# A graph-attention kernel on one core: VectorE makes the destination lanes and codes of two groups of edges at once

## What is computed

```python
def _gat_layer(x, src, dst, W, a_src, a_dst, b, heads, ch, concat):
    n = x.shape[0]
    h = (x @ W).reshape(n, heads, ch)
    alpha_src = jnp.sum(h * a_src, axis=-1)
    alpha_dst = jnp.sum(h * a_dst, axis=-1)
    e = alpha_src[src] + alpha_dst[dst]
    e = jnp.where(e > 0, e, NEG_SLOPE * e)
    alpha = _segment_softmax(e, dst, n)
    msg = h[src] * alpha[:, :, None]
    out = jax.ops.segment_sum(msg, dst, num_segments=n)
    out = out.reshape(n, heads * ch) if concat else out.mean(axis=1)
    return out + b
```

## Time and profile before

| what | value |
|---|---|
| median of 3 runs | 8928.67 us (8913.6 to 8929.7) |
| the profiled execution, whole | 8916.15 us |
| its span, first to last instruction | 8914.5 us |
| first attention layer (4060 to 6440 us of the span) | 2380 us, DVE busy 2269.61 us |
| second attention layer (6560 to 8840 us of the span) | 2280 us, DVE busy 1582.16 us, POOL 1718.94 us |
| mean granted TensorE clock | 0.765 of full speed |

### The profile page before, as it was taken

How to read it: one execution, slowest core, us unless ns; L and a number is a source line. 1 busy time by engine, 2 the same in 40 slices (tenths; PEclk the granted TensorE clock), 3 DMA queues, 4 the chain that set the end, 5 groups by cost and what they waited for, 6 DMA issues and landing times.

```text
span 8914.5 us, 232214 instructions
## 1 busy us (share of the span) xinstructions
PE 6375.9 (72%) x50562; PEld 5197.4 (58%) x50563; DVE 6392.5 (72%) x27688; ACT 4848.8 (54%) x11854; POOL 6136.1 (69%) x7562
## 2 busy tenths in 40 slices
PE   2466666666599999985777777777647777777775
PEld 2366656665588888863444444444445665556664
DVE  7799833333267767757999999999957777777776
ACT  4133333333245555535767667677647777777775
POOL 0377777777777777735777777777637777777775
PEclk9988888888799999986888888888755555555555
DMA  4232222222233333312222222222521111111114
GB/s 141 52 63 62 62 63 62 63 62 62 60 92 85 86 86 85 86 30 59 55 54 55 54 54 55 55 54 54 49 23 28 28 28 28 28 28 28 28 28 27
DMA packets 990660, 491.49 MB, mean 55 GB/s; under 512 B 830674, under 2 KB 841604, under 8 KB 990276
## 3 DMA queue, kind: packets, MB, share of 16 engines
q0 software_dynamic: 168832, 302.29, 15.6%
q1 hardware_dynamic: 701892, 169.48, 10.4%
q10 hardware_dynamic: 119840, 18.68, 1.3%
HBM read 356.53 MB, written 151.48 MB: 57 GB/s over the span
## 4 chain that ended last, share of the span: by engine, by line
issue 25%; DVE 20%; PE 19%; POOL 18%; DMA 7%; ACT 6%; DVEq 3%; ACTq 1%; POOLq 0%; SPq 0%
POOL z_s L637 13%; POOL arena L687 5%; DMA arena<-table,arena 5%; PE ps_all L959 5%; PE ps_all L969 5%; PE ps_all L982 3%; ACT arena L823 3%; PE ps_all L979 2%; DVE shift L1528 2%; DVE arena L1487 2%; DVE arena L1532 2%; PE ps_all L1066 1%; ACT arena L855 1%; DVE arena L1573 1%; DMA z_s<-arena 1%
## 5 line engine op out<-in xcount | busy, mean ns | idle before, releaser
L687 POOL DMA_INDIRECT arena<-table,arena x3616 | 3471.7, 960 | 1504.4 <-issue 982.6
L637 POOL DMA_INDIRECT z_s<-arena x1660 | 1592.1, 959 | 849.9 <-issue 477.5
L1090 PE MATMUL ps_all<-arena 128*128 128x132 f32 (+1 forms) x7232 | 1561.4, 384 | 1.8 <-DVE acc L1590 1.8
L1090 PEld LDWEIGHTS ps_all<-arena 128*128 128x128 f32 x7232 | 1384.9, 284 | 2.7 <-issue 2.6
L823 ACT ACTIVATE arena<-lanes_b,arena 128x128 bf16<-128x128 bf16 x3616 | 1147.1, 387 | 415.6 <-DVE arena L1461 414.4
L1487 DVE TENSOR_REDUCE arena<-ps_all 128x2 f32<-128x1024 f32 x904 | 1098.9, 1216 | 15.5 <-PE ps_all L1107 15.5
L1066 PE MATMUL ps_all<-ident_b,arena 128*128 128x128 bf16 x3616 | 472.3, 273 | 789.1 <-DMA arena<-table,arena 522.6
L1107 PE MATMUL ps_all<-arena,pick 128*128 128x512 bf16 x2260 | 971.0, 523 | 72.5 <-DVE arena L1487 72.1
L847 ACT ACTIVATE arena<-ps_all 28x512 bf16<-28x512 bf16 (+1 forms) x904 | 522.6, 578 | 718.5 <-PE ps_all L1066 718.5
L742 ACT ACTIVATE arena<-ps_all 18x512 f32<-18x512 f32 x415 | 243.3, 586 | 1212.0 <-PE ps_all L946 1192.5
L1066 PEld LDWEIGHTS ps_all<-ident_b,arena 128*128 128x128 bf16 x3616 | 291.1, 120 | 942.7 <-DVE arena L1474 528.8
(11 more groups left out here) (259 smaller groups left out, 16141.0 us busy)
## 6 DMA issues: line engine op xcount, KB each, us to landing
arena<-z_s SPq DMA_DIRECT2D x452, 264.0 KB, 2.7
arena<-table,arena POOLq DMA_INDIRECT x3616
arena<-rec_d SPq DMA_DIRECT2D x1660, 10.0 KB
z_s<-arena POOLq DMA_INDIRECT x1660
rec_d<-in_rec ACTq DMA_DIRECT2D x1, 16160.0 KB, 58.8
arena<-ids_d SPq DMA_DIRECT2D x904, 4.0 KB
arena<-pos_d SPq DMA_DIRECT2D x830, 0.5 KB
arena<-pos_d ACTq DMA_DIRECT2D x830, 0.5 KB
```

The source lines that it names most:

```text
L637: pool.indirect_dma_start(z_s, bass.IndirectOffsetOnAxis(ap=slot[:, g.slot(SLOTS), u:u + 1], axis=0), z_out[:, g.slot(SLOTS), u, :], None) ...
L687: pool.indirect_dma_start(g_rows[:, r, u * step + CODE_WORDS:(u + 1) * step], None, tables[n], bass.IndirectOffsetOnAxis(ap=ids[:, r, 0, u ...
L1090: mm = pe.matmul(ps[6][:, 0:out_w], a_hot_f[:, g.slot(4), u, :], g_msg[:, g.slot(4), u * out_w:(u + 1) * out_w], start=(u == 0), stop=(u = ...
```

## The change

In every second step (when the next group's number inside the turn is odd) `edge_codes` gets two groups, t and t+1 (`ahead = of(-1)`), and each of its operations covers both; in the other steps it does nothing. The two slots lie side by side, so the operations are 128x8, 128x8, 128x128, 128x64 and 128x64. L1458 and L1461 were tensor-with-pointer operations (TENSOR_SCALAR) and become TENSOR_TENSOR, with two columns of `first_node` broadcast along the four columns of a group. Each operation adds two to a semaphore of its own: `a_lane_ready`, `neg_lane_ready`, `bits_ready`, `low_code_ready`, `high_code_ready`. The waits on DVE are those of the later group. SP waits for two semaphores where it waited for one, PE too; ACT waits for `neg_lane_ready`.

```diff
-                        sp.wait_ge(S("a_lane_ready"), g.back(SLOTS).done(2))
+                        sp.wait_ge(S("a_lane_ready"), g.back(SLOTS).done())
+                        sp.sem_inc(S("sp_go"), 1)
+                        sp.wait_ge(S("neg_lane_ready"), g.back(SLOTS).done())
...
-                        act.wait_ge(S("a_lane_ready"), g.done(2))
+                        act.wait_ge(S("neg_lane_ready"), g.done())
...
-                        pe.wait_ge(S("code_ready"), g.done(2))
+                        pe.wait_ge(S("low_code_ready"), g.done())
+                        pe.wait_ge(S("high_code_ready"), g.done())
...
-                def edge_codes(g):
+                def edge_codes(g, h):
...
-                    dve.wait_ge(S(f"ids_in_{r}"), g.uses(SLOTS, 16))
-                    dve.tensor_scalar(lane_int[:, g.slot(4), :], ids[:, r, 1, :], first, None, ALU.subtract).then_inc(S("a_lane_ready"), 1)
-                    if g.back(4).exists():
-                        dve.wait_ge(S("a_hot_ready"), g.back(4).done())
-                    dve.tensor_scalar(neg_lane[:, g.slot(4), :], ids[:, r, 1, :], -1.0, first, ALU.mult, ALU.add).then_inc(S("a_lane_ready"), 1)
+                    first = first_node[:, bass.ds(g.at, 2)].unsqueeze(2).broadcast_to([P, 2, U])
+                    for k in (g, h):
+                        dve.wait_ge(S(f"ids_in_{k.slot(SLOTS)}"), k.uses(SLOTS, 16))
+                    dve.tensor_tensor(lane, node, first, ALU.subtract).then_inc(S("a_lane_ready"), 2)
+                    if h.back(4).exists():
+                        dve.wait_ge(S("a_hot_ready"), h.back(4).done())
+                    dve.tensor_tensor(minus, first, node, ALU.subtract).then_inc(S("neg_lane_ready"), 2)
...
+                    dve.tensor_tensor(bits.rearrange("p k u c -> p (k u) c"),
+                                      lane.rearrange("p k u -> p (k u)").unsqueeze(2).broadcast_to([P, 2 * U, CODE]),
+                                      bit_masks.unsqueeze(1).broadcast_to([P, 2 * U, CODE]), ALU.bitwise_and).then_inc(S("bits_ready"), 2)
...
+                    dve.tensor_scalar(codes[:, :, :, 0:CODE // 2], bits[:, :, :, 0:CODE // 2], 0.0, -BIG, ALU.is_equal, ALU.mult
+                                      ).then_inc(S("low_code_ready"), 2)
+                    dve.tensor_scalar(codes[:, :, :, CODE // 2:CODE], bits[:, :, :, CODE // 2:], 0.0, -BIG, ALU.not_equal, ALU.mult
+                                      ).then_inc(S("high_code_ready"), 2)
...
-                    codes, large, shifts = edge_codes(of(0)), largest_shares(of(3)), new_shifts(of(4))
+                    ahead = of(-1)
+                    codes = edge_codes(of(0), ahead) if ahead is not None and ahead.off % 2 == 1 else iter(())
+                    large, shifts = largest_shares(of(3)), new_shifts(of(4))
```

More of the change, by code:

```diff
@@ L1446, in _ @@
                 buckets = Rounds(dve, mybir.EngineType.DVE, bucket_of, NT - 1, SLOTS, 2 * SLOTS)
-                def edge_codes(g):
+                def edge_codes(g, h):
                     if g is None:
                         return
-                    r = g.slot(SLOTS)
-                    codes = g_rows[:, r, 0:U * step].bitcast(BF16).rearrange("p (u w) -> p u w", u=U)
-                    bits = lane_bits[:, g.slot(4)]
-                    first = first_node[:, bass.ds(g.at, 1)]
-                    dve.wait_ge(S(f"ids_in_{r}"), g.uses(SLOTS, 16))
-                    dve.tensor_scalar(lane_int[:, g.slot(4), :], ids[:, r, 1, :], first, None, ALU.subtract).then_inc(S("a_lane_ready"), 1)
-                    if g.back(4).exists():
-                        dve.wait_ge(S("a_hot_ready"), g.back(4).done())
-                    dve.tensor_scalar(neg_lane[:, g.slot(4), :], ids[:, r, 1, :], -1.0, first, ALU.mult, ALU.add).then_inc(S("a_lane_ready"), 1)
+                    r, q = g.slot(SLOTS), g.slot(4)
+                    codes = g_rows[:, r:r + 2, 0:U * step].bitcast(BF16).rearrange("p k (u w) -> p k u w", u=U)
+                    lane, minus = lane_int[:, q:q + 2], neg_lane[:, q:q + 2]
+                    bits = lane_bits[:, q:q + 2]
+                    node = ids[:, r:r + 2, 1, :]
+                    first = first_node[:, bass.ds(g.at, 2)].unsqueeze(2).broadcast_to([P, 2, U])
[5 more added lines that the diff above has]
+                    dve.tensor_tensor(minus, first, node, ALU.subtract).then_inc(S("neg_lane_ready"), 2)
@@ L1462, in edge_codes @@
                     yield
-                    dve.wait_ge(S("a_lane_ready"), g.done(2))
-                    dve.tensor_tensor(bits, lane_int[:, g.slot(4), :].unsqueeze(2).broadcast_to([P, U, CODE]),
-                                      bit_masks.unsqueeze(1).broadcast_to([P, U, CODE]), ALU.bitwise_and).then_inc(S("bits_ready"), 1)
+                    dve.wait_ge(S("a_lane_ready"), h.done())
+                    dve.tensor_tensor(bits.rearrange("p k u c -> p (k u) c"),
+                                      lane.rearrange("p k u -> p (k u)").unsqueeze(2).broadcast_to([P, 2 * U, CODE]),
+                                      bit_masks.unsqueeze(1).broadcast_to([P, 2 * U, CODE]), ALU.bitwise_and).then_inc(S("bits_ready"), 2)
@@ L1466, in edge_codes @@
                     yield
-                    if g.back(SLOTS).exists():
-                        dve.wait_ge(S("turned"), g.back(SLOTS).done())
-                    dve.wait_ge(S("bits_ready"), g.done())
-                    dve.tensor_scalar(codes[:, :, 0:CODE // 2], bits[:, :, 0:CODE // 2], 0.0, -BIG, ALU.is_equal, ALU.mult
-                                      ).then_inc(S("code_ready"), 1)
-                    dve.tensor_scalar(codes[:, :, CODE // 2:CODE], bits[:, :, CODE // 2:], 0.0, -BIG, ALU.not_equal, ALU.mult
-                                      ).then_inc(S("code_ready"), 1)
+                    if h.back(SLOTS).exists():
+                        dve.wait_ge(S("turned"), h.back(SLOTS).done())
```

1 line of the change is left out of this document (added).

## The result

The changed kernel takes 8903.37 us in the median (8889.92 to 8908.02, 10 runs) against 8928.91 us (10 runs) of the kernel before beside it: a ratio of 0.9973, 95% interval 0.9964 to 0.9981. The forecast was 94 us, and the time lies above the range. The profile after is of an execution of 8889.92 us, the fastest of the ten and 13.5 us under their median.

A forecast was written before the change was run, and what follows sets the result against it. DVE was taken to bound layer one and POOL layer two. 54 turns x (42.14 - 40.4) = 94 us, with 0 from layer two, taken from 8928.67 gave 8835 us; range 8808 to 8879.

The forecast's parts named there:

- The step that loses its codes: Layer one, the DVE step of a pair without codes, lanes and bits: gains 0.50 us, bounds 0.40 to 0.56.
- The stall behind L1522: Layer one, step without codes: a dependent operation follows too closely, so 0.06 us of the gain turn into a stall.
- The step with two groups' codes: Layer one, the DVE step with the wide operations: costs 0.02 us more, bounds -0.06 to +0.16.
- DVE's turn: Layer one, eight steps on DVE: from 42.14 to 40.2 us, between 39.7 and 41.2.
- The part of the turn that is lost at its start stays: Layer one, DVE at the start of a turn: the time lost there is unchanged, while four pairs gain 1.92 us.
- The larger counts: 40.4: Layer one: DVE and POOL ask for nearly the same time, POOL's 40.4 us a turn counts; gain 94 us.
- Layer two: Second attention layer: POOL's turn of 40.4 us stays the bound, DVE has idle time; gain 0 us.
- third rival: POOL's gathers last longer beside DVE's new two-operand operations; sign: gathers over 0.95 us in layer two; slower, chance 0.04.
- The waits that are added: DVE's wait for the later group's ids and second semaphores on PE and SP: cost nothing.
- DVE stays the bound: Rival, layer one: wide operations or stalls cost more, turn 40.65 to 41.2 us, 8849 to 8879 us; chance 0.25.
- Another wait takes the place: Rival, layer one: DVE waits for ACT or PE instead, gain within 18 us, 8911 to 8947 us; chance 0.06.
- The gathers stretch: Rival, POOL: new two-operand DVE operations lengthen gathers; 0.1 us a step takes back 90 us; slower, chance 0.04.

The follow-up runs named there:

- c_one_input: Changed kernel on chip B, message multiplication replaced by a one-input TENSOR_REDUCE, weights left out: 8850.07 us, 0.9954 of the kernel before.
- c_three: Changed kernel on chip B with three gathers for a group in place of four, from a layer's ninth group on: 8386.81 us, one run.
- d_psum: Changed kernel on chip C; ACT writes the exponentials a second time into PSUM, the message multiplication reads its weights there: 9032.41 us, 1.0114 of the kernel before.
- c_halves: Changed kernel on chip B with the message multiplication in two operations of half the elements: 8877.35 us, 0.9985 of the kernel before.
- a_three: Changed kernel on chip A with three gathers for a group in place of four, from a layer's ninth group on: 10375.74 us, one run.
- a_one_input: Changed kernel on chip A, message multiplication replaced by a one-input TENSOR_REDUCE, weights left out: 12249.50 us, 1.0005 of the kernel before.

## Why the prediction was wrong, point by point

**The step that loses its codes: right.** Expected 0.50 us; in the steady part of a turn these steps are 4.55 to 4.61 us in c_one_input, 0.43 to 0.49 under the 5.04 of before. The stall behind L1522 was expected to cost 0.06. The stalls are larger, and partly elsewhere: from start to start L1560 takes 0.11 us for the 0.08 of old, and L1525, ahead of L1592, 0.19 for 0.07 (medians). The old L1535 took 0.13 ahead of the codes and takes 0.07 now, which gives some of it back.

**The step with two groups' codes: right in the middle of the turn.** Timeline of DVE in the changed kernel, around bits, codes and lanes, in the middle of a turn:

```profile
5520.84 0.18 DVE L1479 TENSOR_SCALAR arena<-arena 128x64 bf16<-128x64 int32 x1
5520.94 0.18 DVE L1481 TENSOR_SCALAR arena<-arena 128x64 bf16<-128x64 int32 x1
5521.04 0.14 DVE L1520 TENSOR_SCALAR arena<-dst_parts 128x12 bf16 x1
...
5525.75 0.22 DVE L1464 TENSOR_TENSOR arena<-arena,first_node 128x8 int32<-128x8 int32 x1
5525.89 0.15 DVE L1467 TENSOR_TENSOR arena<-first_node,arena 128x8 f32<-128x8 int32 x1
5525.97 0.16 DVE L1560 TENSOR_TENSOR arena<-arena,ps_all 128x16 f32<-128x16 f32 x1
...
5526.56 0.29 DVE L1470 TENSOR_TENSOR arena<-arena,bit_masks 128x128 int32<-128x128 int32 x1
5526.77 0.16 DVE L1568 TENSOR_TENSOR arena<-arena,ps_all 128x16 f32<-128x16 f32 x1
```

From start to start: codes 0.10 each (expected 0.11), the lanes 0.14 and 0.08 here and 0.10 and 0.08 in the median (0.08), bits 0.21 (0.20). The prices drawn from neighbouring rows held to 0.02 us.

**DVE's turn: 40.8 to 41.0 and not 40.2. This is the first step that failed.** The sum took every pair of the turn for a steady pair. Median step lengths of layer one, from L1520 to L1520:

| step of the turn | 0 | 1 | 2 | 3 | 4 | 5 | 6 | 7 |
|---|---|---|---|---|---|---|---|---|
| before | 5.54 | 4.91 | 5.05 | 5.04 | 5.04 | 5.04 | 5.04 | 6.48 |
| c_one_input | 5.77 | 4.56 | 5.20 | 4.55 | 5.03 | 4.61 | 5.03 | 5.93 |

The steps without codes gave 0.35, 0.49, 0.43 and 0.55, together 1.82 of the 2.00 counted. The others cost +0.23, +0.15 and twice -0.01, together 0.36 where 0.08 was counted, and all of it in steps 0 and 2 (step 2 is at 5.08 in the changed kernel itself). "The part of the turn that is lost at its start stays" was wrong: the stop stays, but in step 0 the lanes save nothing. In the kernel before, behind the stop at 5410.86:

```profile
5411.08 0.16 DVE L1515 TENSOR_TENSOR arena<-arena,alpha_d 128x4 f32<-128x4 f32 x1
5411.32 0.23 DVE L1458 TENSOR_SCALAR arena<-arena,first_node 128x4 int32<-128x4 int32 x1
5411.46 0.22 DVE L1461 TENSOR_SCALAR arena<-arena,first_node 128x4 f32<-128x4 int32 x1
5411.59 0.17 DVE L1553 TENSOR_TENSOR arena<-arena,ps_all 128x16 f32<-128x16 f32 x1
```

In the changed kernel, behind the stop at 5515.24:

```profile
5515.46 0.16 DVE L1522 TENSOR_TENSOR arena<-arena,alpha_d 128x4 f32<-128x4 f32 x1
5515.76 0.17 DVE L1464 TENSOR_TENSOR arena<-arena,first_node 128x8 int32<-128x8 int32 x1
5515.94 0.17 DVE L1467 TENSOR_TENSOR arena<-first_node,arena 128x8 f32<-128x8 int32 x1
5516.05 0.17 DVE L1560 TENSOR_TENSOR arena<-arena,ps_all 128x16 f32<-128x16 f32 x1
```

The first operations behind the stop were slow before as well (L1515 0.24 us, where it takes 0.07 in mid-turn). Now L1522 holds DVE for 0.30 us and L1464 for 0.18. From L1515 to L1553 were 0.51 us, from L1522 to L1560 are 0.59: 0.08 more, where the same change saves 0.10 in mid-turn. What they wait for there, the trace doesn't name. With 40.80 in place of 40.4 the forecast would have been some 22 us smaller; by c_one_input, layer one without held gathers is 66.1 us shorter than in the profile of before, not 94.

**"The larger counts: 40.4": the second failure, and the larger.** It took POOL's turn as a fixed 40.4 us, with every gather at 1.26 us whatever DVE does beside it; a price for gathers that meet the multiplication stood nowhere in the sum. 71.2 us of held time against 22.0 is the row that says no; c_one_input puts its price at 46.7 us in layer one and 8.7 in layer two, 51 us of the median. With the 28 us of the step before that is 79 us for 69 missing. The two prices come from different chips and single profiles; where the 10 us too many belong isn't shown.

**Layer two: 0, and it was +6.3 us.** POOL was its bound, as said, and that is why nothing hides a held gather there. With 128x256 elements the multiplication occupies DVE for 0.34 us and holds a gather by up to 0.2: between 6600 and 8700 us 64 gathers of the changed kernel start 0.1 or 0.2 us behind it (median durations 1.14 and 1.04), and none of the kernel before. That is the sign that the prediction had named for its third rival, gathers longer than 0.95 in layer two.

**The waits that are added: nothing, right.** No wait of DVE for ids stands in the table of waits of layer one.

**The rivals.** *DVE stays the bound* described layer one half-way: its 40.65 to 41.2 us is DVE's turn as c_one_input and c_three show it, but in the changed kernel POOL, and not DVE, sets the turn. *Another wait takes the place* failed: L1580 never waits for ACT in the changed kernel. *The gathers stretch* was the right mechanism with the wrong actor and the wrong price. The prediction looked at the new operations with two SBUF operands, of 0.08 to 0.2 us; they hold little (of 69 gathers that start during L1470 in layer one, three take over 1.0 us; in c_one_input 12 of 67, at most 1.07). The one that holds the gathers is the old message multiplication, which the change doesn't touch. And it dismissed the rival with "the gathers take 0.95" of layer two, although has 1.04 and 1.07, and the trace of before has 22 gathers over 1.1 us and a longest of 1.47 in layer one. Each of the 22, and the 1.07, started 0.5 us or less behind L1573; the 1.04 started 0.09 us behind L1585, another operation with two operands in SBUF. That one look, at the longest gather rather than at the usual one, would have shown what a gather costs that starts at the wrong time, and that the change takes away the even step that kept the others out of it.

The Trainium skill ("SBUF — State Buffer", section "Who interferes with whom") states the rule that the prediction had weighed: a DVE instruction with two inputs in SBUF and a GpSimd instruction that reads SBUF exclude each other. This case's runs agree in one direction: a gather that starts during the multiplication takes up to 1.51 us for 0.95 with two inputs in SBUF, 0.95 to 0.96 with one (c_one_input) or with the other in PSUM (d_psum). In the other direction they show nothing: with a gather under way the multiplication takes 0.60 us from its start to the next, as without one.

## What to carry to other kernels

When a change makes an engine's steps uneven or shortens them, look at how its long operations with two SBUF operands lie against the gathers of POOL, and read the longest gathers, not the median. A gain measured on one chip can be none on another: here it was 25 us in two comparisons and nothing in the third. Two engines whose periods match can be locked in a harmless position, and the profile before then shows nearly nothing of what a slide costs. A loop's first steps are to be priced by their own rows, since there a saving can vanish that is real in the steady steps.

## What the runs showed of the hardware that was not expected

- The multiplication holds a gather only if it *starts* while the multiplication runs, and by that operation's rest (1.48 us at 0.03 us behind it, 1.34 at 0.19). A gather that is under way is not disturbed (0.95 us at 5524.51). Two such operations in a row act as one: 1.57 us.
- Two operands in SBUF are not the whole condition. The wide code operations L1479 and L1481 of the changed kernel have one, and of 45 gathers that start during L1479 in layer one 22 take over 1.0 us. POOL, then DVE:

```profile
4245.59 1.09 POOL L689 DMA_INDIRECT arena<-table,arena  x1 [0.30 <-issue]
```

```profile
4245.56 0.18 DVE L1479 TENSOR_SCALAR arena<-arena 128x64 bf16<-128x64 int32 x1
4245.66 0.18 DVE L1481 TENSOR_SCALAR arena<-arena 128x64 bf16<-128x64 int32 x1
4245.76 0.15 DVE L1520 TENSOR_SCALAR arena<-dst_parts 128x12 bf16 x1
```

  The gather is 0.14 us too long, held until about the end of L1481. The price here is small, 2.8 us in layer one; why these operations hold it wasn't tested.
- In layer two of the changed kernel DVE stops for some 4 us at the start of a turn (4.05 in the median, 1.47 before). Timeline of DVE, starts of steps:

```profile
7417.18 0.17 DVE L1520 TENSOR_SCALAR arena<-dst_parts 128x3 bf16 x1
...
7426.93 0.17 DVE L1520 TENSOR_SCALAR arena<-dst_parts 128x3 bf16 x1 [4.40 <-issue]
...
7431.29 0.16 DVE L1520 TENSOR_SCALAR arena<-dst_parts 128x3 bf16 x1
...
7434.11 0.16 DVE L1520 TENSOR_SCALAR arena<-dst_parts 128x3 bf16 x1
```

  The queue that brings instructions moved 329 packets in the whole of that execution, and 65 before (the page's third part, changed, then before):

```profile
q14 instruction: 329, 2.70, 0.1%
```

```profile
q14 instruction: 65, 0.53, 0.0%
```

  264 more is about 5 for each of the 54 turns of one layer. The stop is there in every run of the changed kernel, and with one input or three gathers (329 packets each), and in neither the runs with halves nor d_psum (65), which differ from it by a few instructions. Alone it costs nothing while POOL is the bound (c_one_input has it, and 2286.4 us in layer two, as before). But DVE then makes up for it in steps of 3 to 4 us, and in these the gathers of layer two meet the multiplication: 51 of the 78 gathers that take over 1.0 us in this loop lie in the second step behind the stop. c_halves, without the stop, has none over 1.02 us, the changed kernel 18 over 1.1. Why a few instructions decide it isn't shown.
- The time depends on the chip by more than the change: 8891 (B), 8927 (C) and 8929 us (the comparison of the result) for the kernel before, and 12244 (A) and 12278 (D). On A and D DVE and PE stop in every second step; what stops them was not followed up, but in a_three, with three gathers for four, layer one has hardly any such stop. The stage ahead of the attention layers is slower there too: layer one's first gather starts at 5016 us (a_one_input), where it starts at 4062 in the changed kernel's profile.
